# Weighted sums of an attention in one burst of twelve tiles per half batch, and a context buffer refilled chunk by chunk

## What is computed

```python
C_q = Q @ Wq_d
C_kv = K @ Wkv_d                                   # K: context, 1500 x 512 per batch; C_kv: 1500 x 32
CqWqk = (C_q @ W_qk).reshape(b, n, H, LKV)         # 16 heads of 32
scores = jnp.einsum('bnhl,bkl->bhnk', CqWqk, C_kv) / jnp.sqrt(LKV)
attn = jax.nn.softmax(scores, axis=-1)
V_up = (C_kv @ Wv_u).reshape(b, nkv, H, HD)
out = jnp.einsum('bhnk,bkhd->bnhd', attn, V_up)
```

## Time and profile before

| | before |
|---|---|
| median of 3 runs | 698.24 us |
| profiled execution, first to last instruction | 696.1 us |
| TensorE busy | 608.3 us, 87% |
| VectorE busy | 463.0 us, 67% |
| ScalarE busy | 318.8 us, 46% |
| GpSimd busy | 424.5 us, 61% |
| mean granted TensorE clock | 0.956 of full |
| HBM read | 59.19 MB |

### The profile page before, as it was taken

How to read it: one execution, slowest core, us unless ns; L and a number is a source line. 1 busy time by engine, 2 the same in 40 slices (tenths; PEclk the granted TensorE clock), 3 DMA queues, 4 the chain that set the end, 5 groups by cost and what they waited for, 6 DMA issues and landing times.

```text
span 696.1 us, 12998 instructions
## 1 busy us (share of the span) xinstructions
PE 608.3 (87%) x3856; PEld 327.8 (47%) x3856; DVE 463.0 (67%) x773; ACT 318.8 (46%) x697; POOL 424.5 (61%) x394
## 2 busy tenths in 40 slices
PE   4868898898899898898899898899899898985975
PEld 3335554454456354454456445455456445442322
DVE  2716785588758966588758966588758966754452
ACT  1421063547444645337444654437444654463450
POOL 5002055588658877288658877288648876699400
PEclk9986898999999999999999999999999999998897
DMA  8776510551018110551028100651028100100000
GB/s 316 228 270 259 199 35 1 197 206 42 1 49 317 69 25 2 216 203 42 1 68 320 51 20 1 221 198 42 1 78 313 51 18 1 47 9 1 22 1 13
DMA packets 29820, 72.32 MB, mean 104 GB/s; under 512 B 16049, under 2 KB 23569, under 8 KB 27314
## 3 DMA queue, kind: packets, MB, share of 16 engines
q1 hardware_dynamic: 29586, 70.37, 29.6%
q10 hardware_dynamic: 160, 1.05, 0.4%
HBM read 59.19 MB, written 2.88 MB: 89 GB/s over the span
## 4 chain that ended last, share of the span: by engine, by line
PE 52%; DVE 16%; issue 9%; POOL 7%; ACT 5%; DVEq 0%; POOLq 0%; ACTq 0%
PE mx_ps L671 8%; PE st_ps L641 7%; POOL acc L1093 7%; PE pv_ps L656 6%; PE mi_ps L443 4%; DVE mx_p L1017 4%; PE mi_ps L437 3%; PE mi_ps L496 3%; PE mi_ps L450 3%; PE mi_ps L553 2%; PE mi_ps L623 2%; DVE xn L893 2%; PE mi_ps L627 2%; PE mi_ps L521 2%; PE mi_ps L525 2%
## 5 line engine op out<-in xcount | busy, mean ns | idle before, releaser
L1093 POOL TENSOR_TENSOR acc<-acc,p_ring 125x448 f32<-125x448 f32 x300 | 359.5, 1198 | 49.0 <-ACT p_ring L828 23.4
L1017 DVE TENSOR_REDUCE mx_p<-mx_ps 128x1 f32<-128x500 f32 x336 | 210.3, 670 | 84.5 <-PE mx_ps L671 83.1
L828 ACT ACTIVATE p_ring<-st_ps 125x448 f32<-125x448 f32 x384 | 190.0, 544 | 139.5 <-PE st_ps L641 133.5
L641 PE MATMUL st_ps<-q_st,c_st 98*125 98x448 f32 x384 | 153.6, 429 | 12.0 <-ACT p_ring L828 7.5
L671 PE MATMUL mx_ps<-c_st,q_st 96*128 96x500 f32 x336 | 139.1, 445 | 5.6 <-DVE mx_p L1017 5.4
L641 PEld LDWEIGHTS st_ps<-q_st,c_st 98*125 98x125 f32 x384 | 68.6, 190 | 109.5 <-ACT p_ring L828 85.8
L1101 POOL TENSOR_TENSOR rstd<-mv,eps_col 128x1 f32<-128x1 f32 x24 | 4.5, 190 | 166.1 <-DVE mv L889 166.1
L656 PE MATMUL pv_ps<-p_ring,c_nat 125*32 125x448 f32 x768 | 94.7, 566 | 1.1 <-ACT p_ring L828 0.9
L671 PEld LDWEIGHTS mx_ps<-c_st,q_st 96*128 96x128 f32 x336 | 63.0, 196 | 31.0 <-DVE mx_p L1017 17.1
L953 DVE TENSOR_TENSOR q_st<-mi_ps,q_st 32x224 fp32r<-32x224 f32 x64 | 22.2, 384 | 53.8 <-ACT q_st L739 53.4
L1093 POOL TENSOR_TENSOR acc<-p_ring 125x448 f32<-125x448 f32 x30 | 36.6, 1221 | 31.3 <-ACT p_ring L828 31.3
(11 more groups left out here) (111 smaller groups left out, 688.8 us busy)
## 6 DMA issues: line engine op xcount, KB each, us to landing
ctx_sb<-in_ctx_t SPq DMA_DIRECT2D x16, 3000.0 KB, 10.7
c_st<-ct_hl SPq DMA_DIRECT2D x192, 46.9 KB, 2.0
x_sb<-in_x SPq DMA_DIRECT2D x16, 112.0 KB
out_y<-x3n SPq DMA_DIRECT2D x16, 112.0 KB
wq_sb<-in_wq SPq DMA_DIRECT2D x2, 512.0 KB, 4.5
ctx_sb<-in_lora_a SPq DMA_DIRECT2D x1, 1024.0 KB, 7.0
ctx_sb<-in_lora_b SPq DMA_DIRECT2D x1, 1024.0 KB, 8.9
wo_sb<-in_wo SPq DMA_DIRECT2D x1, 1024.0 KB, 17.3
```

The lines of the kernel that those rows point to most:

```text
L641: mm(st_ps[unit % STB][0:KC, 0:HALF], c_st[:, b % 4, t * KT + k * KC:t * KT + (k + 1) * KC], q_st[:, b // 2 % 2, b % 2, half * HALF:(half ...
L828: act.activation(p_ring[:, unit % PR, :], st_ps[unit % STB][0:KC, 0:HALF], ACT.Exp, scale=float(L) ** -0.5).then_inc(exp_done, 1)
L1017: ve.tensor_reduce(mx_p[:, p:p + 1], mx_ps[unit % MXB][:, 0:KP], AX.X, ALU.max).then_inc(red_done, 1)
L1093: po.tensor_tensor(dst, first, p_ring[:, unit % PR, :].rearrange("p (h s) -> p h s", s=S), ALU.add).then_inc(acc_done, 1)
```

## The change

`sums` is called once per half batch, behind the second score of the group that follows the half, and issues 3 x 4 matmuls in a row instead of 4 in each of three groups. The exps of a whole half batch must therefore be kept: `p_ring` has 16 tiles instead of 8. The room comes from `ctx_sb`, which has one slot instead of two. Each of its four chunks has its own DMA and semaphore, and is loaded for the next batch when the latents of this batch have read it: SP issues chunks 0 and 1 behind Ah and chunks 2 and 3 behind A. TensorE waits per chunk. The raw low-rank factors, which were kept in the second slot before the loop, now lie in `p_ring`, so the second context load no longer waits for them and is issued ahead of the first spread of C.

```diff
-PR = 8
+PR = 16
+UNITS = 4 * KG
-        ctx_sb = sb("ctx_sb", [128, 2, CH, NK])
+        ctx_sb = sb("ctx_sb", [128, CH, NK])
-        p_ring = sb("p_ring", [KC, PR, HALF])
+        p_ring = sb("p_ring", [128, PR, HALF])
-        spare = ctx_sb[:, 1, :, :].rearrange("p c k -> p (c k)")
+        spare = p_ring[:, :, :].rearrange("p a b -> p (a b)")
...
-        ctx_in = [sem(f"ctx_in{n}", 16) for n in range(2)]
+        ctx_in = [sem(f"ctx_in{c}", 32) for c in range(CH)]
+        ctx_free = sem("ctx_free", 2 * (CH - 1))
...
-            def load_ctx(b):
-                if b >= 2:
-                    sp.wait_ge(ps["A"], due(ps["A"], b - 1))
-                dma(ctx_sb[:, b % 2, :, :],
-                    ctx_t[batch_index(b)].rearrange("(p c) k -> p c k", c=CH)).then_inc(ctx_in[b % 2], 16)
+            def load_ctx(b, chunks):
+                for c in chunks:
+                    if b and c < CH - 1:
+                        sp.wait_ge(ctx_free, due(ctx_free, (CH - 1) * (b - 1) + c + 1))
+                    elif b:
+                        sp.wait_ge(ps["A"], due(ps["A"], b))
+                    dma(ctx_sb[:, c, :],
+                        ctx_t[batch_index(b)].rearrange("(p c) k -> p c k", c=CH)[:, c, :]).then_inc(ctx_in[c], 16)
...
+            load_ctx(1, range(CH))
             spread_ct(0)
-            sp.wait_ge(lora_ps, due(lora_ps, 8))
-            load_ctx(1)
...
                 if 2 * i + 2 < B:
                     load_x(i + 1)
-                    load_ctx(2 * i + 2)
                 for g in range(2 * GROUPS):
                     for name, n in steps_of(i, g):
-                        if name == "A":
+                        if name == "Ah" and n + 1 < B:
+                            load_ctx(n + 1, (0, 1))
+                        elif name == "A":
+                            if n + 1 < B:
+                                load_ctx(n + 1, (2, 3))
                             spread_ct(n)
-                            if n % 2 and n + 2 < B:
-                                load_ctx(n + 2)
...
-            def latents(o, slot, chunks):
+            def latents(n, o, chunks):
                 for c in chunks:
+                    pe.wait_ge(ctx_in[c], due(ctx_in[c], 16 * (n + 1)))
                     for t in range(4):
                         last = mm(o[t * L:(t + 1) * L, 0:KT], wkv_sb[:, c, :],
-                                  ctx_sb[:, slot, c, t * KT:(t + 1) * KT], start=(c == 0), stop=(c == CH - 1))
+                                  ctx_sb[:, c, t * KT:(t + 1) * KT], start=(c == 0), stop=(c == CH - 1))
+                        if t == 3 and c < CH - 1:
+                            last.then_inc(ctx_free, 1)
...
-            def sums(b, g):
-                half, k = g // KG, g % KG
-                pe.wait_ge(exp_done, due(exp_done, b * 24 + g * 4 + 4))
-                if g == 0:
+            def sums(b, half):
+                pe.wait_ge(exp_done, due(exp_done, b * 24 + half * UNITS + UNITS))
+                if half == 0:
                     pe.wait_ge(ct_sb, due(ct_sb, b + 1))
-                if k == 0 and b * 2 + half:
+                if b * 2 + half:
                     pe.wait_ge(ox_sb, due(ox_sb, b * 2 + half))
-                for t in range(4):
-                    unit = b * 24 + g * 4 + t
-                    last = mm(pv_ps[t * L:(t + 1) * L, 0:HALF], c_nat[:, b % 4, k, t * L:(t + 1) * L],
-                              p_ring[:, unit % PR, :], start=(k == 0), stop=(k == KG - 1))
+                for k in range(KG):
+                    for t in range(4):
+                        unit = b * 24 + half * UNITS + k * 4 + t
+                        last = mm(pv_ps[t * L:(t + 1) * L, 0:HALF], c_nat[:, b % 4, k, t * L:(t + 1) * L],
+                                  p_ring[0:KC, unit % PR, :], start=(k == 0), stop=(k == KG - 1))
                 last.then_inc(pv_done, 1)
...
-                        if t == 1 and 0 <= bl < B:
-                            sums(bl, gl)
+                        if t == 1 and gl % KG == KG - 1 and 0 <= bl < B:
+                            sums(bl, gl // KG)
...
-                        act.wait_ge(pv_done, due(pv_done, old // 4 + 1))
+                        act.wait_ge(pv_done, due(pv_done, old // UNITS + 1))
```

More of the change, by code:

```diff
@@ L196, in decoder_layer @@
         gkron = sb("gkron", [128, PAIRS, 8])
-        spare = ctx_sb[:, 1, :, :].rearrange("p c k -> p (c k)")
+        spare = p_ring[:, :, :].rearrange("p a b -> p (a b)")
         lora_raw = [spare[:, 0:2048], spare[:, 2048:4096]]
-        lora_eff = [p_ring[0:64, :, :].rearrange("p a b -> p (a b)"),
-                    acc[0:64, :, :, :].rearrange("p a h s -> p (a h s)")]
+        lora_eff = [spare[0:64, 4096:6144], acc[0:64, :, :, :].rearrange("p a h s -> p (a h s)")]
         st_ps = [bank(f"st_ps{n}") for n in range(STB)]
@@ L214, in decoder_layer @@
         x_in = [sem(f"x_in{n}", 16) for n in range(2)]
-        ctx_in = [sem(f"ctx_in{n}", 16) for n in range(2)]
+        ctx_in = [sem(f"ctx_in{c}", 32) for c in range(CH)]
+        ctx_free = sem("ctx_free", 2 * (CH - 1))
         ab_in = sem("ab_in", 32)
-        for s in x_in + ctx_in:
+        for s in x_in:
             rates[s.name] = 32
@@ L246, in decoder_layer @@
         exp_done = sem("exp_done", 48)
-        pv_done = sem("pv_done", 12)
+        pv_done = sem("pv_done", 4)
         ox_sb = sem("ox_sb", 4)
@@ L383, in _ @@
             dma(g8[:, :], gate_t).then_inc(raw_in, 16)
-            load_ctx(0)
+            load_ctx(0, range(CH))
             dma(wo_sb[:, :, :], wo.rearrange("(r p) n -> p r n", p=128)).then_inc(w_out, 16)
@@ L560, in step @@
                         pe.wait_ge(s1_sb, due(s1_sb, 2 * n + 3))
-                    pe.wait_ge(ctx_in[slot], due(ctx_in[slot], 16 * (n // 2 + 1)))
-                    latents(o, slot, (0, 1))
+                    latents(n, o, (0, 1))
                     return
                 elif name == "A":
-                    last = latents(o, slot, (2, 3))
+                    last = latents(n, o, (2, 3))
                 elif name == "CT":
@@ L825, in exponentials @@
                     if old >= 0:
-                        act.wait_ge(pv_done, due(pv_done, old // 4 + 1))
+                        act.wait_ge(pv_done, due(pv_done, old // UNITS + 1))
                         act.wait_ge(acc_done, due(acc_done, old // 12 * ADDS + max(old % 12, 1)))
-                    act.activation(p_ring[:, unit % PR, :], st_ps[unit % STB][0:KC, 0:HALF], ACT.Exp,
+                    act.activation(p_ring[0:KC, unit % PR, :], st_ps[unit % STB][0:KC, 0:HALF], ACT.Exp,
                                    scale=float(L) ** -0.5).then_inc(exp_done, 1)
             def out_of_sums(b, half):
-                act.wait_ge(pv_done, due(pv_done, b * 6 + half * KG + KG))
+                act.wait_ge(pv_done, due(pv_done, b * 2 + half + 1))
                 if b % 2 == 0 and half == 0 and b:
@@ L1006, in add_up_last @@
                         if k == 1:
-                            first = p_ring[:, (unit - 1) % PR, :].rearrange("p (h s) -> p h s", s=S)
+                            first = p_ring[0:KC, (unit - 1) % PR, :].rearrange("p (h s) -> p h s", s=S)
                         else:
@@ L1010, in add_up_last @@
                             first = dst
-                        ve.tensor_tensor(dst, first, p_ring[:, unit % PR, :].rearrange("p (h s) -> p h s", s=S),
+                        ve.tensor_tensor(dst, first, p_ring[0:KC, unit % PR, :].rearrange("p (h s) -> p h s", s=S),
                                          ALU.add).then_inc(acc_done, 1)
@@ L1092, in add_up @@
                             first = dst
-                        po.tensor_tensor(dst, first, p_ring[:, unit % PR, :].rearrange("p (h s) -> p h s", s=S),
+                        po.tensor_tensor(dst, first, p_ring[0:KC, unit % PR, :].rearrange("p (h s) -> p h s", s=S),
                                          ALU.add).then_inc(acc_done, 1)
```

## The result

| kernel | runs | median | ratio to before, 95% interval | profiled span |
|---|---|---|---|---|
| before | 4 | 697.4 us | | 696.1 us |
| after | 4 | 725.9 us (721.4 to 727.4) | 1.0407 [1.0355, 1.0459] | 724.7 us |

The median of before is 697.4 us here, since a fourth run (691.3 us) came to the three. Medians take in all runs of a kernel; the ratios leave out a run more than 1.5% above its kernel's fastest.

What follows compares the result with a forecast made beforehand. TensorE, 87% busy, paces only some stretches; other engines hold the rest. Terms 16.5 - 0.95 + 0.7 + 2.1 - 0.4 gave +18 us on the 696.1 us span, plus 2.1 us around it: 716 us, range 704 to 726.

Steps and rivals of the forecast that it cites:

- start, up to body 0's first score: First latents begin with the last score add instead of waiting for the one 3 MB context load: -0.4 us.
- body 0: Scores one batch, in groups 6 to 11; its first burst was in group 7: 0.15 - 0.8 - 0.3 = -0.95 us.
- bodies 1 to 6: Steady bodies, each two batches in 12 score groups numbered 0 to 11: +2.75 us each, +16.5 in all.
- body 7: Paced by GpSimd's row of sums up to T3: +1.5 us from group 0, -0.8 from group 11, together +0.7.
- body 8: Only scores the last batch: four groups save 0.6 us each, two long bursts and the final sums pay 1.5 each: +2.1.
- The price of a burst: Twelve sums in a row in groups 0, 3, 6, 9: two further sets of four add 1.5 us, bounds 1.26 and 1.78.
- Groups 2, 7 and 8: Groups without their burst start the fourth score earlier: 0.8 us saved in 2, 0.3 in 7, 0.8 in 8.
- Groups 1, 4, 5, 10 and 11: Losing their burst gains 0: VectorE holds 1, 4, 10 and 11, ScalarE holds 5.
- Group 9: Its long burst runs beside VectorE's stretch; only 0.15 us of it was put on the path.
- Context and ring: Context by chunks, refilled once read, and a deeper ring of exps: hidden in the loop, 0 us.
- The doubt with bounds 0 and 7 us: Chunks 0 and 1 issued just before the spread of maxima that group 6 needs: 0 to 1 us a body, taken as 0.
- rival C: Maxima land behind context chunks, group 6 waits 1 to 2 us a body, idle lowers the clock: 723 to 730 us; chance 0.16.

Runs made afterwards that it cites:

- kernel 1: After with the sums called as before, four per group; ring of 16 tiles and chunked context stay. 698.1 us, ratio to before 1.0038.
- kernels 1 to 8: The first eight follow-up kernels, all built on after, with sums placed differently or unread matmuls added; medians from 688.4 to 719.0 us.
- kernel 3: Kernel 1 with only the sums of groups 10, 11 and 0 in one burst, in group 0. 718.7 us, ratio to before 1.0372.
- kernel 5: Kernel 1 with only the sums of groups 4, 5 and 6 in one burst, in group 6. 716.5 us, ratio to before 1.0265.
- kernel 6: Kernel 1 with only the sums of groups 1, 2 and 3 in one burst, in group 3. 704.6 us, ratio to before 1.0136.
- kernel 2: Kernel 1 with only the sums of groups 7, 8 and 9 in one burst, in group 9. 691.8 us, ratio to before 0.9965.
- kernel 4: After with four unread matmuls behind the second score of groups 4, 5, 11 and the last body's groups 1, 2, 4, 5. 719.0 us, ratio to before 1.0332.
- kernel 7: Kernel 2 with group 3 emptied too, its set moved to group 4 and group 4's own ahead of MT. 692.7 us, ratio to before 0.9924.

## Why the prediction was right, and where it was too low

The mechanism was right and one size was off: the sum had no term for the granted clock. The lengths of the bodies in the two profiles (from the first score of each to the next), and what of the difference I put down to the clock, by stretches that took more or less time at the lower level than in before:

| term | forecast | measured | of it the clock |
|---|---|---|---|
| start, up to body 0's first score | -0.4 | +3.0 | 2.8 |
| body 0 | -0.95 | -4.9 | -2.4 |
| bodies 1 to 6 | +16.5 | +23.0 | 5.7 |
| body 7 | +0.7 | +2.0 | 1.2 |
| body 8 | +2.1 | +5.5 | 3.1 |
| sum | +18 | +28.6 | 10.4 |

The 5.7 are +3.1 and +2.8 from MT to the end of bodies 3 and 4, +1.7 from group 6 to W1 in body 1 (17.18 us against 15.46 in the others), less 0.3 and 1.6 in group 0 of bodies 1 and 3, where before had the lower level and after had less of it or none. The clock of the first two rows is not the bursts' doing: ahead of body 0 it was after that ran slower (matmuls on constants at 28.51 us took 3.63 us, 1.93 in before), in body 0 it was before (37.5 us, where kernel 1 takes 34.4), and the two nearly undo each other. It comes and goes from run to run: in the traces of kernels 1 to 8, whose code up to there is after's, body 0's first score stands anywhere from 90.6 to 93.7 us. Without the last column 18.2 us are left where 18 were forecast. That this is so close is luck in part, since misses cancel: body 0 is 1.5 us under its forecast, bodies 1 to 6 are 0.8 above, the start 0.6 and body 8 0.3.

1. The price of a burst, 1.5 us: right, 1.50 in group 0 (kernel 3), 1.5 in group 6 at full clock (kernel 5), 0.8 with group 2's gain in group 3 (kernel 6).
2. Groups 2, 7 and 8: -0.8 for group 2 measured -0.7 (T1 to its fourth score in body 6 2.32 us, 3.02 before), -1.1 for 7 and 8 together measured -0.93 (kernel 2).
3. Groups 1, 4, 5, 10 and 11 held by other engines: right. xn ended at 465.88 + 1.37 = 467.25 in body 5, T1 started at 467.30, the 0.05 us of the earlier trace rows; MT stood at unchanged distances behind S and, in the mean of six bodies, behind W1.
4. Group 9, +0.15: 0.
5. Body 0: groups 10 and 11 are not held there. Group 6 to W1 is 11.82 us and W1 to MT 16.75, against 13.27 and 17.77 in kernel 1 at the same clock, so -1.45 and -1.0 for -1.1 and +0.15. I had applied the steady body's VectorE row to a body in which VectorE has less to do (W1 to MT in kernel 1: busy 11.8 us in body 0, 15.0 in body 6).
6. Body 7: group 0 to T3 52.14 us before and 53.91 after, +1.8 for +1.5. T3 to F1 4.56 and 3.52, -1.0 for -0.8. F1 to the end 5.02 and 6.27: the clock.
7. Body 8: two bursts 1.4 and 1.5 us longer than 2.46 and two pairs of scores 0.27 us further apart make 3.4 of clock; from the last T3 to the end after took 13.0 us and before 13.5, so 3.1 in all. The other 2.4 were forecast as 2.1.
8. Context and ring, 0: right in the steady bodies (76.65 us in kernel 1 for 76.55); in the median they cost 0.4%, whose source isn't shown. The spread of the maxima behind two chunks did not hold up group 6:

```profile
ctx_sb<-in_ctx_t SPq DMA_DIRECT2D x64, 750.0 KB, 6.3
```
```profile
486.29 1.17 SPq L342 DMA_DIRECT2D ctx_sb<-in_ctx_t  x2
488.54 1.60 SPq L367 DMA_DIRECT2D q_st<-m_t  x2
```

A chunk lands in 6.3 us, where the whole load took 10.7. MT started at 487.85 and group 6 at 493.56, 5.7 us apart as in before. Only in body 7 one score waited for that DMA (1.27 us at 640.56), where MT to group 6 was still 0.5 us shorter than before. The doubt with bounds 0 and 7 us was worth 0: the two chunks ahead of the spread had landed by 492.5 us, before group 6 needed it, so the rule on a ring's order, weighed for it, can't be told from its opposite here. The margin is thin all the same: of 60 steady bodies in the ten traces with a context by chunks, group 6 waited for this DMA in two (0.77 us in body 2 of kernel 6, 0.61 in body 4 of kernel 4). The spread of C, whose small DMAs now stand right behind two chunks, does come later: 4.0 us to landing in the median where before took 2.0, and 3.6 to 4.0 in the nine experiments with chunks. The first one of body 5, issued at 465.40, landed at 471.68, behind the first of the two chunks (470.56) and ahead of the second (474.31). Body 6 of kernel 1 shows no cost of it. The rows of after and of before:

```profile
c_st<-ct_hl SPq DMA_DIRECT2D x192, 46.9 KB, 4.0
```
```profile
c_st<-ct_hl SPq DMA_DIRECT2D x192, 46.9 KB, 2.0
```

The step that failed is in rival C, which had the two causes in one: "the maxima land behind the context chunks ... and longer idle stretches in groups 4 and 5 lower the granted clock". Its first half was wrong and its second right, in groups 10 and 11 and body 8 rather than 4 and 5, so that the median lies in C's 723 to 730 us for half of C's reasons: it had put 1 to 2 us a body on the maxima, which cost nothing, and the clock cost about 10. At 0.16 for both together it stood outside the sum, and it should have been a term of it: the trace of before already showed what an idle stretch costs, F1 at 1.97 us behind the last T3's wait and 1.09 elsewhere. The misses of kernels 3 and 5 (7.7 and 9.5 us) came for the most part from the same gap in the same direction, and for the rest from body 8's own burst. The Trainium skill (TensorE: Matmul & The Clock Gate, HAM oscillation — how this bites in real kernels) warns that idle gaps of TensorE cost the speed of the work behind them; the traces agree, and here already single waits of 0.97 us (MT in body 3) and at most 1.4 us (the scores, by the table of waits) stood ahead of the slow stretches.

What stays open: why body 6 of after kept the clock behind the same idle time that cost bodies 3 and 4 some 3 us each. Idle time alone doesn't tell: TensorE was busy 5.5 of the 8 us ahead of MT in bodies 4 and 6 of after, of which one lost the clock, and 5.3 to 5.8 in kernel 3, where all six did. I can't forecast in which body it falls.

## What to carry to other kernels

Where groups of work are held by different engines, a merged burst is paid in full where TensorE's own work decides and is free only beside another engine's row: price each place by itself, and put the bursts into the waits, not where the loop is simplest. Idle time that is given to TensorE off the critical path is not free: multiply the matmuls that stand behind it by the price of the lower clock before calling a wait harmless. A few matmuls that nobody reads, in a wait just ahead of a row of matmuls that sets the end, can pay for themselves.

## What the hardware did that I had not expected

- Each kernel's runs spread with the clock: after took 721.4 us at a clock of 0.950 and 726.7 at 0.941, and kernel 7 686.2 us at 0.965 and 695.6 at 0.948.
- Behind short waits, each between matmuls (0.7 us ahead of the scores and 0.97 ahead of MT in body 3 of after), the clock fell from 2.4 to 1.2 GHz, in kernel 3 in all of bodies 1 to 6; with fillers in them (kernel 4) it did not fall at that place.
- Three sets of four column-tiled matmuls in a row cost 2.39 us, and one cost 0.89: adjacency saves 0.14 us for each further set beyond the 0.24 us of getting in and out, so a merge by itself has little to give.
- Small DMAs issued just behind two loads of 750 KB on the same queue landed in 4.0 us in the median instead of 2.0 (3.6 to 4.0 in the nine experiments with the same loads).
